# Output projection, norm, MLP and logits of a two-layer transformer in one program over eight blocks; attention without its loop

## The reference

```python
y = jnp.einsum('bhij,bhjv->bhiv', a, v)          # a = softmax(q k), 16 heads of 32
y = y.transpose(0, 2, 1, 3).reshape(b, l, d)
x = x + y @ wo
h2 = layer_norm(x, mlp_ln_scale)
h2 = jax.nn.gelu(h2 @ w1) @ w2                   # w1 512x2048, w2 2048x512
x = x + h2
...
att = inputs @ attention_weights                 # second layer: inputs = x, 512x16
att = att - jnp.max(att, axis=1, keepdims=True)
```

## Time and profile before

| | us |
|---|---|
| median of three runs | 3886.65 (3883.5 to 3889.67) |
| the profiled execution | 3881.74 |
| its span, first to last instruction | 3879.9 |
| PE busy | 3463.9 (89% of the span) |
| DVE, ACT, POOL busy | 2037.3, 1529.4, 2111.9 |
| mean granted share of the PE clock | 0.942 |

### The profile page before, as it was taken

The page is one execution under the profiler, slowest core; times in us unless marked ns, Lnnn a source line. Parts: engine busy times, 40 slices in busy tenths (PEclk is TensorE's granted clock), DMA queues, the critical chain, the costliest instruction groups (busy, mean ns, idle before and its releaser), DMA issues. The chain is left out here.

```text
span 3879.9 us, 47864 instructions
## 1 busy us (share of the span) xinstructions
PE 3463.9 (89%) x16544; PEld 2271.6 (59%) x16544; DVE 2037.3 (53%) x3268; ACT 1529.4 (39%) x2795; POOL 2111.9 (54%) x1675
## 2 busy tenths in 40 slices
PE   7997899989999899989999456699979996999997
PEld 5775445544554445544554145588858884777776
DVE  5764777767777677767775155111111113344443
ACT  2331466656666566656666222211111112121121
POOL 2654378876879688886988412122212223454553
PEclk9998999999999899999999777799989997999999
DMA  5556677858686677858655555211011103221220
GB/s 188 173 158 169 123 145 131 154 103 148 131 149 137 110 147 133 157 109 143 135 115 115 135 186 192 92 44 44 33 55 44 44 33 126 78 79 58 86 76 37
DMA packets 146742, 438.11 MB, mean 113 GB/s; under 512 B 15936, under 2 KB 16448, under 8 KB 120384
## 3 DMA queue, kind: packets, MB, share of 16 engines
q1 hardware_dynamic: 123456, 267.22, 25.7%
q0 software_dynamic: 23040, 167.78, 22.4%
HBM read 171.49 MB, written 95.42 MB: 69 GB/s over the span
## 5 line engine op out<-in xcount | busy, mean ns | idle before, releaser
L680 DVE TENSOR_REDUCE part_max<-ps_att 128x1 f32<-128x512 f32 x1972 | 1228.5, 684 | 432.5 <-PE ps_att L601 432.1
L723 ACT ACTIVATE probs<-ps_att 128x512 f32<-128x512 f32 x2048 | 1064.8, 603 | 522.2 <-PE ps_att L575 461.5
L774 POOL TENSOR_TENSOR prob_sums<-prob_sums,probs 128x512 f32<-128x512 f32 x896 | 1159.2, 1568 | 24.5 <-DMA probs<-probs 24.5
L575 PE MATMUL ps_att<-q_stack,k_stack 97*128 97x512 f32 x2048 | 873.1, 429 | 40.9 <-PEq L53 24.2
L601 PE MATMUL ps_att<-k_stack,q_stack 96*128 96x512 f32 x1972 | 788.6, 400 | 0.0
L575 PEld LDWEIGHTS ps_att<-q_stack,k_stack 97*128 97x128 f32 x2048 | 392.1, 192 | 532.0 <-ACT probs L723 359.9
L623 PE MATMUL ps_att<-probs,v_tok 128*32 128x512 f32 x4096 | 548.1, 607 | 0.0
L1362 POOL TENSOR_TENSOR ml_g_lo<-ml_g,ml_g_hi 128x512 fp32r<-128x512 f32 x128 | 164.8, 1288 | 653.5 <-DVE ml_g_hi L1338 653.5
L601 PEld LDWEIGHTS ps_att<-k_stack,q_stack 96*128 96x128 f32 x1972 | 380.7, 193 | 68.1
L1338 DVE CAST ml_g_hi<-ml_g 128x512 fp32r<-128x512 f32 x128 | 54.7, 427 | 570.0 <-ACT ml_g L1296 570.0
L756 POOL DMA_DIRECT2D probs<-probs x160 | 152.9, 956 | 307.6 <-PE ps_att L623 301.4
(11 more groups left out here) (186 smaller groups left out, 4803.7 us busy)
## 6 DMA issues: line engine op xcount, KB each, us to landing
probs<-probs POOLq DMA_DIRECT2D x160, 1024.0 KB, 8.5
q_stack<-qk SPq DMA_DIRECT2D x186, 128.0 KB, 7.1
k_stack<-qk SPq DMA_DIRECT2D x42, 512.0 KB, 11.4
qk<-rot_hi SPq DMA_DIRECT2D x64, 256.0 KB, 3.4
qk<-rot_lo SPq DMA_DIRECT2D x64, 256.0 KB, 2.6
av_gate_rows<-gate SPq DMA_DIRECT2D x64, 256.0 KB
x_in_sb<-in_x SPq DMA_DIRECT2D x8, 1024.0 KB, 8.8
v<-v_stage SPq DMA_DIRECT2D x8, 1024.0 KB, 5.1
```

The costliest lines, as they stand in the source:

```text
L575: nc.tensor.matmul(sT[u % 3], t["kS"][0:S3 + 1, b, h, k * P:(k + 1) * P], t["qS"][0:S3 + 1, h, n * TB:(n + 1) * TB], start=True, stop=True)\
L680: nc.vector.tensor_reduce(t["pm"][:, r, k:k + 1], mx[mx_uses % 3], AX.X, ALU.max)\
L723: nc.scalar.activation(t["p"][:, at % PR, h, :], sT[(at * G + h) % 3], ACT.Exp)\
L774: nc.gpsimd.tensor_tensor(x, first, t["p"][:, w % PR, h, :], ALU.add).then_inc(s["acc_done"], 1)
```

## The change

Two parts.

**Attention.** The loop over the groups goes: `attend` writes out all four groups (8 units of 64 steps) as one block, with one clear ahead and one meeting of the engines behind. Steps, buffers and the order inside a unit stay. What a pass did at its end (POOL's last two rounds, `last_sums`) now stands in the first steps of the next unit.

**One stage for projection, norm, MLP and logits.** `project_out`, `prepare_out`, `mlp` and `split_weights` are replaced by `feed_forward`: one block over all eight blocks of tokens, without loops. wo, w1 and w2 stay on chip, split. Turn n = -1 projects and norms block 0; turn n does the MLP of block n, and beside it the projection and norm of block n+1 and the transposes and logits of block n-1; turn 8 has only the last of these. The normed rows stay in SBUF (x is normed in place, the PE transposes are split straight from PSUM), so h2T in DRAM goes; x1 is still stored and loaded again (into z, which is then both addend and result). The layer-norm scale is multiplied into w1 when that is split. Buffers become smaller: one y piece of 128 tokens instead of two blocks, one GELU buffer instead of two, one zT piece. PSUM: 4 banks for z, 2 for up, and 2 that all of projection, transposes and logits share in turn. The logits are done in two halves of 256 tokens.

```diff
-        with nc.Fori(0, NG - 1) as g:
-            attend_groups(nc, c, a, g, s, t, ps)
-        attend_groups(nc, c, a, NG - 1, s, t, ps, nexts=(True, False))
+        attend(nc, c, a, s, t, ps)
...
+AT_TURN, AT_LOGITS = (1, 2, 4, 6), (3, 8)
+AT_OUT = (5, 7, 9, 11)
+AT_ROOT = 13
+WOUT, WQ = DC, 4
+CHUNKS = DC + 2 * MC
...
+        def chunks_at(n, m):
+            if n == -1:
+                return [m] if 4 <= m < WOUT + 2 * WQ else []
+            first = WOUT + 2 * WQ + 2 * m
+            return [i for i in (first, first + 1) if i < CHUNKS] if n == 0 else []
...
+                def load_chunk(i):
+                    if i >= 4:
+                        sp.wait_ge(s["w_lo"], i - 3)
+                    sp.dma_start(z[:, i % 4, :], chunk(i)[0]).then_inc(s[f"wq_in{i % 4}"], 16)
...
+                def load_y(n, j):
+                    v = n * TT + j
+                    cols = slice(v * P, (v + 1) * P)
+                    if v:
+                        sp.wait_ge(s["y_lo"], v)
+                    sp.dma_start(yr[:], y_v[:, :, cols]).then_inc(s["y_in"], 16)
+                    for f in range(DC):
+                        src = a["rl"][f * G:(f + 1) * G, cols].unsqueeze(1).broadcast_to([G, KD, P])
+                        sp.dma_start(rt[:, f, :], src).then_inc(s["y_in"], 16)
...
+                for n in turns:
+                    for m in range(MC):
+                        if m == 0 and n >= 1:
+                            store_z(n - 1)
+                        if m == 0 and n >= 0 and n + 1 < NA:
+                            load_x(n + 1)
+                            load_y(n + 1, 0)
+                        if n >= 1 and m in AT_TURN:
+                            store_zT((n - 1) * TT + AT_TURN.index(m))
...
+                        if n + 1 < NA:
+                            if m + 1 in AT_OUT[:-1]:
+                                load_y(n + 1, AT_OUT.index(m + 1) + 1)
+                            if m in AT_OUT:
+                                store_x1(n + 1, AT_OUT.index(m))
+                        for i in chunks_at(n, m):
+                            if i + 4 < CHUNKS:
+                                load_chunk(i + 4)
+                        if m == AT_ROOT and 0 <= n < NA:
+                            load_x1(n)
...
+            @block.tensor
...
+                for n in turns:
+                    inside, ahead = 0 <= n < NA, n + 1 < NA
+                    for m in range(MC):
+                        if inside:
+                            up(n, m)
+                        if m == MC - 1 and ahead:
+                            for j in range(2):
+                                turn("tb", (n + 1) * TT + j, x, "xn")
+                        if inside and m:
+                            down(n, m - 1)
+                        if n >= 1 and m in AT_TURN:
+                            turn("tz", (n - 1) * TT + AT_TURN.index(m), z, "z")
+                        if n >= 1 and m in AT_LOGITS:
+                            logits((n - 1) * 2 + AT_LOGITS.index(m))
+                        if ahead and m in AT_OUT:
+                            project((n + 1) * TT + AT_OUT.index(m))
+                    if ahead:
+                        for j in range(2, TT):
+                            turn("tb", (n + 1) * TT + j, x, "xn")
+                    if inside:
+                        down(n, MC - 1)
...
+            @block.scalar
...
+                        if inside:
+                            u = n * MC + m
+                            act.wait_ge(s["u"], u + 1)
+                            if u:
+                                act.wait_ge(s["g_lo"], u)
+                            nc.scalar.activation(gf[:], ps[:, 4 + u % 2, :], ACT.Gelu_apprx_tanh).then_inc(s["g"], 1)
+                        if n >= 1 and m in AT_TURN:
+                            keep_zT((n - 1) * TT + AT_TURN.index(m))
+                        if ahead and m + 1 in AT_OUT:
+                            y_hi((n + 1) * TT + AT_OUT.index(m + 1))
+                        if ahead and m == AT_ROOT:
+                            root(n + 1)
+                        for i in chunks_at(n, m):
+                            chunk_hi(i)
+                    for j in range(TT if ahead else 0):
+                        v = (n + 1) * TT + j
+                        act.wait_ge(s["tb"], v + 1)
+                        nc.scalar.activation(hh[:, :, j * P:(j + 1) * P], by_features("tb", v), ACT.Copy)\
+                            .then_inc(s["h_hi"], 1)
...
+            @block.gpsimd
...
+                            nc.gpsimd.tensor_tensor(gl[:, u % 2, :], gf[:], gh[:, u % 2, :].bitcast(F32), ALU.subtract)\
+                                .then_inc(s["g_lo"], 1)
+                        if n + 1 < NA and m + 2 in AT_OUT:
+                            v = (n + 1) * TT + AT_OUT.index(m + 2)
+                            pool.wait_ge(s["y_in"], 16 * (DC + 1) * (v + 1))
+                            nc.gpsimd.tensor_tensor(yr[:], yr[:], rt[:], ALU.mult).then_inc(s["y_n"], 1)
```

More of the change, by code:

```diff
@@ L427, in _, with plan, attend @@
                 rotated_lo(NA * QK - 1)
-def plan(halves, nexts):
+def plan():
     steps = []
-    for half, b in enumerate(halves):
+    for unit in range(UNITS):
+        b = unit % B
         for w in range(STEPS):
             j = w + AHEAD
-            job = (b, j) if j < STEPS else (1 - b, j - STEPS) if nexts[half] else None
-            steps.append({"half": half, "b": b, "w": w, "n": w // LT, "k": w % LT, "job": job})
-    return steps
-def attend_groups(nc, c, a, g, s, t, ps, halves=(0, 1), nexts=(True, True)):
-    steps = plan(halves, nexts)
+            job = (b, j) if j < STEPS else (1 - b, j - STEPS) if unit + 1 < UNITS else None
+            steps.append({"unit": unit, "b": b, "w": w, "n": w // LT, "k": w % LT, "job": job})
+    return steps
+def attend(nc, c, a, s, t, ps):
+    steps = plan()
     o_ps, l_ps = ps[:, 0, :], ps[:, 1, :]
@@ L447, in attend_groups @@
     mx = [ps[:, 5 + i, :] for i in range(3)]
-    blocks = len(halves) * NB
+    blocks = UNITS * NB
     ends = [at for at, st in enumerate(steps) if st["job"] and st["job"][1] % JOBS == JOBS - 1]
@@ L521, in _ @@
                     load_q(g, b, NB - 1)
-                if nexts[st["half"]]:
+                if unit + 1 < UNITS:
                     if w in K_AT or w in V_AT:
@@ L579, in wait_stacks @@
             def wait_stacks(st):
-                half = st["half"]
+                unit = st["unit"]
                 b, j = st["job"]
@@ L614, in values @@
                 n, k = w // LT, w % LT
-                half = steps[w]["half"]
+                unit = steps[w]["unit"]
                 pe.wait_ge(s["exp"], G * (w + 1))
@@ L618, in values @@
                     pe.wait_ge(s["o_kept"], n)
-                if half and w % STEPS == 0:
-                    pe.wait_ge(s["v_in"], 32 * half)
+                if unit and w % STEPS == 0:
+                    pe.wait_ge(s["v_in"], 32 * unit)
                 for h in range(G):
@@ new lines, in feed_forward @@
+        awr, lns = sb("aw_raw", [P, DC, H2]), sb("ln_scale_sb", [P, DC])
+        x, z = sb("ff_x", [P, TT, D]), sb("ff_z", [P, TT, D])
+        yr, rt = sb("ff_y", [P, DC, P]), sb("ff_rl", [P, DC, P])
+        yh, yl = sb("ff_y_hi", [P, DC, P], F32R), sb("ff_y_lo", [P, DC, P], F32R)
+        hh, hl = sb("ff_h_hi", [P, DC, TB], F32R), sb("ff_h_lo", [P, DC, TB], F32R)
+        gf = sb("ff_g", [P, TB])
+        gh, gl = sb("ff_g_hi", [P, 2, TB], F32R), sb("ff_g_lo", [P, 2, TB], F32R)
+        zf = sb("ff_zT", [P, DC, P])
@@ new lines, in feed_forward, with chunk @@
+        s = {n[3:]: v for n, v in s.items()}
+        x_v, x1_v, z_v = (a[n].rearrange("(n j p) f -> n p j f", n=NA, p=P) for n in ("x", "x1", "z"))
+        l_v, r_v = (a[n].rearrange("h (c t) -> (h c) t", t=TB) for n in ("lS", "rl"))
+        y_v = a["yT"].rearrange("(k p) t -> p k t", p=P)
+        one_over = zf[:].rearrange("p f t -> p (f t)")
+        turns = range(-1, NA + 1)
+        def chunk(i):
+            if i < WOUT:
+                return a["wo"][:, i, :], woh[:, i, :], wol[:, i, :], None
+            q, r = (i - WOUT) // (2 * WQ), (i - WOUT) % (2 * WQ)
+            if r < WQ:
+                cols = slice(q * D, (q + 1) * D)
+                return a["w1"][:, r, cols], w1h[:, r, cols], w1l[:, r, cols], lns[:, r:r + 1]
+            m = q * WQ + r - WQ
+            return a["w2"][:, m, :], w2h[:, m, :], w2l[:, m, :], None
@@ new lines, in _ @@
+                        if ahead and m == AT_ROOT:
+                            normed(n + 1)
+                        for i in chunks_at(n, m):
+                            chunk_lo(i)
+                    for j in range(TT if ahead else 0):
+                        v = (n + 1) * TT + j
+                        cols = slice(j * P, (j + 1) * P)
+                        dve.wait_ge(s["h_hi"], v + 1)
```

(3 more changed lines are left out.)

744 lines of the change are left out of this document (285 added, 459 removed).

## The result

The median is 3702.85 us (3697.58 to 3706.48, four runs) against 3885.07 us before (3882.91 to 3889.67): a ratio of 0.9528, 95% interval 0.9511 to 0.9546, or 182 us less. The forecast was 3685 us, 200 less. The profiled execution took 3699.31 us.

What follows compares the result with a forecast made beforehand. PE was taken to decide in all three stages, through its standing and low-clock stretches. Terms -62 (attention), -213.6 (prologue) and +74.3 (MLP) sum to -201.3: 3680.4 us profiled, 3685 us median, range 3655 to 3745.

Steps and rivals of the forecast that it cites:

- Attention, -62: Attention without its loop: three loop ends gone (58.0 us) and 4 us less excess in second blocks, minus 62 us.
- The loop ends, 58.0: Attention: the three loop ends become inner block ends, whose last step takes 4.0 us instead of 24.3, 24.6 and 21.1.
- I take 4 over three passes: Attention: stall excess of each pass's second block goes between not at all and entirely; 4 us taken as saved.
- Rival 2: Attention unit boundaries: the 9.9 us wait for POOL is backlog and stays, with the stalls; +34 us, 3719; chance 0.07.
- Prologue, 287.8 to 74.2: From attention to first MLP matmul: four y pieces in turn through one buffer, 74 us instead of 288, minus 213.6.
- 29, 31, 5.1 and 8.5: Prologue, us: first projection's start, the fourth's delay after it, its low-clock run, then add through norm, turns and copies.
- MLP, 868.7: First MLP matmul to the last stage's first: units, projections, transposes, logits, tail and late copies; 868.7 us, plus 74.3.
- 128 units of 5.443: MLP: 128 units of 24 matmuls at the old kernel's pace, 5.443 us each, 696.7 us in all.
- late copy: Beginning of each MLP block: ACT's second copy can come late behind queued DMAs, logits 0.5 us later; 3.5 us.
- Rival 1: Prologue and blocks: y piece loads decide; +84 us (3769) at 15.4 us a load, 4154 at 30.8; chance 0.09.
- rival 3: MLP blocks: the square root's table loads lie on PE's path, 18 us more, 3703; chance 0.03.
- rival 4: Longer straight code waits for instructions at 28 more block ends, +200 us, no change; chance 0.02 including the unforeseen.

Runs made afterwards that it cites:

- k_later: The change with two of a pass's six K loads issued at steps 22 and 38 instead of 18 and 22; median 3687.12 us.
- ends: The change with two sets of buffers for block 0's y pieces and the last block's transposed z in the idle x tile; median 3691.61 us.
- ff_all32: The change with the layer-norm scale tile moved behind the others, so weights and activations both start at 32 modulo 64; median 3691.88 us.

## Why the prediction was right, and where it was off

- **Attention, -62: -50 in the profile, -47 on average.** The loop ends, 58.0, were right (57.7). The step that failed is "I take 4 over three passes" for the excess of the second blocks: I let it go down, and it went up, by 8 in the profile and by 11 on average. The stalls come from pair DMAs of POOL that land late among the loads of a pass's start (`k_later`); these met before too, and why they cost PE more now stays open. I had bounded the term by "not at all" and "entirely" and left out that it could grow. Rival 2 (a backlog of POOL stays at the boundaries) is out: the last step of a pass takes 3.9 us. That POOL now has less room in the blocks behind it is what the rows leave as a reading for the stalls.
- **Prologue, 287.8 to 74.2: 75.7.** All of its mechanism held: one y buffer sets the pace (`ends` shows it), the weight splits hide between the pieces. A load took 8.5 to 9.3 us instead of 7, a piece 11.2 to 12.0 instead of 10.4, and the first piece came 2 us earlier. (The terms as written, 29, 31, 5.1 and 8.5, add up to 73.6 and not to the 74.2 that was taken off.)
- **MLP, 868.7: 879.1.** Term by term: units 716.8 instead of 696.7 (+20.1), low clock at the start 2.3 (-0.5), projections 28 x 2.80 = 78.4 (+0.3), transposes 22.4 instead of 30.8 (-8.4; the 32 of a block take 3.2, where I had taken twice the 2.19 of the earlier trace rows, which holds a wait of PE behind the first eight), logits 2.89 a block or 20.2 (-0.8), tail 37.6 instead of 35.8 (+1.8), late copy 0 (-3.5), and 1.4 not attributed. The step that failed is "128 units of 5.443": I carried a matmul's duration over from the old MLP as a constant of the operation. The earlier trace rows held the warning: 12 logit matmuls in 2.79 us are 0.2325 each beside the MLP's 0.2268, and I used both numbers without asking why they differed. (Those logits' tiles lay alike, with a stationary side of 16 columns; their pace stays unexplained.) "Inside the MLP PE is gapless" holds for an inner block only: at the turn of the old loop a block takes 122.9 instead of 92.2 us. The 794.4 us contain these 30.7, and the sum was right to leave them out, since it was built from the parts.
- **Rival 1** (load of the pieces) is out at 8.6 us inside a block against 13 free; **rival 3** (table loads) at ten loads a block; **rival 4** (waiting for straight code) by 841.56 us of PE without a gap and by pass ends of 3.9 us.
- The marks: first up-projection 75.7 us after the attention (60 to 95 allowed), blocks 107.07 us apart (106 to 107 said; with the slower units alone it would have been 108.7, the transposes and the copy gave the difference back), PE busy over 98% and at full clock. The one mark missed was the attention's end, 2118.8 for 2112.
- 3702.85 lies in the stated 3655 to 3745, and the two errors that matter, +12 and +20, had the same sign; -8 for the transposes hid a part of them. That the median is the very number given for rival 3 (3703) is chance: its table loads cost nothing.

## What to carry to other kernels

When a stage is rewritten, a matmul's duration from the old stage is an estimate, not a constant: list the start addresses of what PE reads, modulo 64, before and after, and put small tiles behind the large ones, or pad, so that stationary and moving side stay alike. When a loop is written out, its drains go, and with them idle time that may have absorbed something: look for DMAs that land late in the first blocks, and spread the loads around them. A table load, a buffer or a DMA costs what it is late by, so read the idle time of its engine first; here 80 table loads cost nothing, and one missing set of y buffers 15 us.

## What the runs showed of the hardware

- A matmul of 512 columns with fp32r operands takes 0.2268 us at full clock when both SBUF tiles start alike modulo 64 bytes, and 0.2333 when one starts at 0 and the other at 32, whichever it is: four combinations, over 400 matmuls of each kind of the MLP in the window, no gap between them. Why, the traces don't show. In the first stage 0.231 to 0.235 was seen with alike addresses as well.
- Matmuls of 256 columns (16 stationary ones) take 0.117 us from start to start and fp32 transposes of 128 columns 0.109, the latter both in the change (identity and z at 0) and in `ff_all32` (z at 32).
- A pair addition of 1 MB by DMA landed after 8.5 us in the median, after 17.2 beside six q loads (128 KB each) and the K load (512 KB) of step 18, and after 13.2 without that K load (one pair each, in the third pass).
- The same attention code took 1693.6 to 1708.5 us in eight profiles, and the same last stage 617.3 to 628.0 in ten; an MLP block without any wait of PE repeated to 0.02 us.
